# Turning ternary weight halves one at a time, and loading attention values earlier, in a two-layer transformer kernel

## The reference, cut to what matters

```python
xn = layernorm(x)
q, k = rope(xn @ wq), rope(xn @ wk)        # 16 query heads, 4 key heads of 128
s = softmax(mask(q @ k.T / sqrt(128))) @ v @ wo   # window of 64 keys and the first 32
gu = xn @ ternary(w_gate_up).T             # scale and sign per group of 64 weights
f = rms_norm(silu(gate) * up) @ ternary(w_proj).T
x = x + s * silu(f)
# then the second block: 16 heads of 16 over all 512 keys, and a GELU network in f16 products
```

## Time and profile before

| | us |
|---|---|
| median of 3 runs | 818.72 (818.72 to 818.73) |
| profiled execution, its own time | 823.13 |
| span of the profiled execution, first to last instruction | 821.3 |
| PE busy | 771.0 (94% of the span) |
| DVE, ACT, POOL busy | 607.8, 474.4, 299.4 |
| units of the first repetition (29.2 to 128.4): span | 99.2 |
| of it PE, DVE, ACT, POOL busy | 78.81, 79.54, 76.16, 67.73 |

### The profile page before, as it was taken

One profiled execution on the slowest core, in us unless ns is written; L12 is line 12 of the kernel. 1 busy time (PEld: TensorE's weight loads), 2 busy tenths in 40 slices (PEclk: granted clock), 3 DMA queues, 4 the chain that ended last, 5 costly groups with the idle time before them and its releaser, 6 DMA issues.

```text
span 821.3 us, 13360 instructions
## 1 busy us (share of the span) xinstructions
PE 771.0 (94%) x4656; PEld 476.8 (58%) x4656; DVE 607.8 (74%) x1632; ACT 474.4 (58%) x968; POOL 299.4 (36%) x255
## 2 busy tenths in 40 slices
PE   4869879989999999999999999999999999999996
PEld 2546568736446667856436667865445666774543
DVE  6949877758857677888957678687967667677862
ACT  3769764443777664143796775133696776233483
POOL 1348861122008885002006886001103888100201
PEclk9979989999999999999999999999999999999999
DMA  9131002184003120057002210028101300017400
GB/s 296 62 85 52 1 27 84 52 233 103 3 11 102 35 63 1 1 159 201 3 2 63 75 59 14 1 102 235 26 2 37 88 27 1 1 48 216 98 3 26
DMA packets 56818, 55.37 MB, mean 67 GB/s; under 512 B 14256, under 2 KB 43312, under 8 KB 56752
## 3 DMA queue, kind: packets, MB, share of 16 engines
q1 hardware_dynamic: 52768, 49.63, 21.3%
q10 hardware_dynamic: 3664, 3.84, 1.7%
q0 software_dynamic: 320, 1.05, 0.4%
HBM read 39.00 MB, written 15.24 MB: 66 GB/s over the span
## 4 chain that ended last, share of the span: by engine, by line
PE 68%; issue 11%; DVE 10%; ACT 4%; DMA 3%; POOL 2%; SPq 1%; ACTq 0%; POOLq 0%; DVEq 0%
PE bank L923 14%; PE bank L1034 7%; PE bank L958 6%; PE bank L1241 5%; PE bank L1225 5%; PE bank L1020 5%; PE bank L1136 4%; PE bank L1164 4%; PE bank L1208 3%; PE bank L1001 3%; PE bank L969 3%; PE bank L1213 2%; PE bank L983 2%; DVE mx L1597 1%; ACT region L760 1%
## 5 line engine op out<-in xcount | busy, mean ns | idle before, releaser
L1597 DVE TENSOR_REDUCE mx<-bank 128x1 f32<-128x512 f32 x256 | 161.1, 683 | 29.0 <-PE bank L1164 24.3
L603 POOL TENSOR_TENSOR region<-region 128x512 f32<-128x512 f32 x75 | 99.8, 1330 | 148.0 <-DVE region L1415 143.3
L923 PE MATMUL bank<-xnT,wrope 128*128 128x512 f32 x320 | 147.2, 603 | 3.3 <-ACT xnT L730 1.2
L875 ACT ACTIVATE region<-bank 128x512 f32<-128x512 f32 x256 | 132.9, 602 | 25.5 <-PE bank L1213 24.0
L760 ACT ACTIVATE region<-region,nb 128x128 f32<-128x128 f32 x256 | 81.5, 390 | 54.6 <-DVE nb L1427 54.3
L599 POOL TENSOR_TENSOR region<-region,sin_sb 128x512 f32<-128x512 f32 x60 | 84.5, 1408 | 41.7 <-ACT region L743 41.1
L923 PEld LDWEIGHTS bank<-xnT,wrope 128*128 128x128 f32 x320 | 58.7, 194 | 65.6 <-issue 61.5
L632 POOL TENSOR_TENSOR region<-region,bo_bc 128x256 f32<-128x256 f32 x16 | 11.7, 729 | 205.4 <-DVE region L1476 205.4
L1408 DVE TENSOR_TENSOR region<-bank,cos_sb 128x512 f32<-128x512 f32 x80 | 54.3, 686 | 36.5 <-PE bank L923 36.1
L741 ACT ACTIVATE region<-bank 64x512 f32<-64x512 f32 x80 | 47.6, 595 | 52.1 <-DVE region L1408 41.4
L958 PE MATMUL bank<-region 128*128 128x128 f32 x512 | 74.2, 290 | 1.6 <-ACT region L755 1.6
(11 more groups left out here) (144 smaller groups left out, 1347.7 us busy)
## 6 DMA issues: line engine op xcount, KB each, us to landing
wrope<-in_wrope SPq DMA_DIRECT2D x80, 128.0 KB, 2.2
scratch<-region SPq DMA_DIRECT2D x16, 512.0 KB, 5.2
Qp<-scratch SPq DMA_DIRECT2D x56, 128.0 KB, 3.6
Kp<-scratch SPq DMA_DIRECT2D x56, 128.0 KB, 3.9
scratch<-region SPq DMA_DIRECT2D x16, 256.0 KB, 5.6
X<-in_x SPq DMA_DIRECT2D x4, 512.0 KB, 4.1
out<-X SPq DMA_DIRECT2D x16, 128.0 KB, 2.0
VW<-v_rows SPq DMA_DIRECT2D x16, 102.0 KB, 2.8
```

The costliest lines, as they stand in the source:

```text
L603: nc.gpsimd.tensor_tensor(dst, dst, tiles(sw[:, r % 2, :], i), ALU.add)\
L875: nc.scalar.activation(P1[:, n % 8, :], turned_bank(n)[:, :], ACT.Exp, scale=SCALE1)\
L923: mm = nc.tensor.matmul(misc(b, name)[:, 0:width], lhs(c), xnT[:, c, :], start=(c == 0), stop=(c == DC - 1))
L1597: nc.vector.tensor_reduce(mx1[:, g % 2, column:column + 1], scores_bank(m)[:, :], AX.X, ALU.max)\
```

## The change

Everything lies in the first repetition; the amount of work is the same on every engine.

- The twelve half pieces were turned in pairs, in units 1, 3, 5, 8, 10 and 13. Now they are turned in eleven units, singly but for one pair: 0, 1, 3 (two), 6, 7, 9, 10, 11, 12, 13, 14.
- The sixteen gate and up products were dealt to units 4 to 13. Now they go to units 3 to 14: gate 0 in unit 3, up 0 in 4, gate 1 in 5, up 1 in 6, gate 2 and up 2 in 7, gate 3 in 8, none in 9, up 3 in 10, and the pairs 4 to 7 in units 11 to 14. So the bank turns change, too. PE's wait for turned weights is split: gate 0 and gate 4 wait for the two halves of their own piece, up 0 and up 4 for theirs.
- On SP, `load_piece(5)` with its wait stands behind the load of rotary weights 14 instead of 9, and so behind `load_windows`.
- On ACT, the four key copies of group 0 are no longer made behind the five swaps, `prepare(1)` and the halving of `bo`: the first is made ahead of swap 3, the second ahead of swap 4, the other two behind it. `key_windows` becomes `key_window`, which makes one copy; in other groups the four are made together as before.

```diff
     for s in range(NKV * TT):
         jobs += [("rope", r) for r in rope_at(s)] + ffn_at(b, s) + ([("ot", 0)] if s == OT_UNIT else [])
-        if b == 0 and s in TURN_UNITS:
-            jobs += [("wt", 2 * TURN_UNITS.index(s) + half) for half in range(2)]
+        jobs += [("wt", k) for k in TURN_AT.get(s, ())] if b == 0 else []
...
-FFN_FIRST = [0, 0, 0, 0, 1, 1, 2, 2, 1, 1, 2, 2, 2, 2, 0, 0]
+FFN_FIRST = [0, 0, 0, 1, 1, 1, 1, 2, 1, 0, 1, 2, 2, 2, 2, 0]
...
-TURN_UNITS = (1, 3, 5, 8, 10, 13)
+TURN_AT = {0: (0,), 1: (1,), 3: (2, 3), 6: (4,), 7: (5,), 9: (6,), 10: (7,), 11: (8,), 12: (9,), 13: (10,), 14: (11,)}
...
-                    if b == 0 and r == 9:
+                    if b == 0 and r == 14:
                         load_piece(5)
...
-            def key_windows(b, g):
-                act.wait_ge(rope_done.sem, rope_done.at(b, 5 * g + 1))
-                if g:
-                    act.wait_ge(s_full.sem, s_full.at(b, TT * g))
+            def key_window(b, g, k):
+                if k == 0:
+                    act.wait_ge(rope_done.sem, rope_done.at(b, 5 * g + 1))
+                    if g:
+                        act.wait_ge(s_full.sem, s_full.at(b, TT * g))
...
-            front(0)
+            xnT_copies(0)
+            for r in range(5):
+                if r >= 3:
+                    key_window(0, 0, r - 3)
+                swap(0, r)
+            for k in range(2, TT):
+                key_window(0, 0, k)
...
-                    for half in range(2) if b == 0 and s in TURN_UNITS else ():
-                        turned_weights(TURN_UNITS.index(s), half)
+                    for k in TURN_AT.get(s, ()) if b == 0 else ():
+                        turned_weights(k // 2, k % 2)
...
-                            if b == 0 and i % 4 == 0 and kind == "gate":
-                                pe.wait_ge(wt_freed.sem, wt_freed.at(0, 4 * (i // 4) + 4))
+                            if b == 0 and i % 4 == 0:
+                                pe.wait_ge(wt_freed.sem, wt_freed.at(0, 4 * (i // 4) + (2 if kind == "gate" else 4)))
...
-                    for half in range(2) if b == 0 and s in TURN_UNITS else ():
-                        turn_weights(TURN_UNITS.index(s), half)
+                    for k in TURN_AT.get(s, ()) if b == 0 else ():
+                        turn_weights(k // 2, k % 2)
```

More of the change, by code:

```diff
@@ L744, in swap @@
                     .then_inc(swap_done.sem, 1)
-            def key_windows(b, g):
-                act.wait_ge(rope_done.sem, rope_done.at(b, 5 * g + 1))
-                if g:
-                    act.wait_ge(s_full.sem, s_full.at(b, TT * g))
+            def key_window(b, g, k):
[3 more added lines that the diff above has]
+                        act.wait_ge(s_full.sem, s_full.at(b, TT * g))
                 keys = kT[:, g % 2, :]
-                for k in range(SPAN // QT):
+                if k < SPAN // QT:
                     src = keys[:, WIN + k * QT:WIN + k * QT + NWIN * QT].rearrange("p (n j) -> p n j", j=QT)
-                    nc.scalar.activation(kW[:, :, k * QT:(k + 1) * QT], src, ACT.Copy).then_inc(kw_ready.sem, 1)
-                front = keys[:, 0:FRONT].unsqueeze(1).broadcast_to([P, NWIN, FRONT])
-                nc.scalar.activation(kW[:, :, SPAN:P], front, ACT.Copy).then_inc(kw_ready.sem, 1)
+                    dst = kW[:, :, k * QT:(k + 1) * QT]
+                else:
+                    src = keys[:, 0:FRONT].unsqueeze(1).broadcast_to([P, NWIN, FRONT])
+                    dst = kW[:, :, SPAN:P]
+                nc.scalar.activation(dst, src, ACT.Copy).then_inc(kw_ready.sem, 1)
             def exps(b, u):
@@ L808, in _ @@
                     if s < NKV * TT:
-                        if s % TT == 0:
-                            key_windows(b, s // TT)
+                        for k in range(TT) if s % TT == 0 and (b or s) else ():
+                            key_window(b, s // TT, k)
                         for r in rope_at(s) if s == 0 else ():
```

## The result

| | before | after |
|---|---|---|
| median of 5 runs, us | 818.73 (818.72 to 821.08) | 815.04 (814.35 to 816.61) |
| ratio of the times, 95% interval | | 0.9937 (0.9917 to 0.9958) |
| profiled execution, own time | 823.13 | 815.04 |
| its span | 821.3 | 813.2 |
| start of unit 0 to the projection | 99.2 | 90.5 |

The change makes the kernel faster by 0.6%: by the ratio 5.2 us (3.4 to 6.8), by the medians 3.7. The forecast was 812.3, within 809.4 to 817.0. The two profiled executions differ by 8.1, which is more than the change is worth; why, the first experiment shows.

The account below looks back on a forecast made before the run. DVE was taken to pace the units, with PE's stalls costing its waits. Unit 4 earlier 3.3, gate 0 0.6 and fewer waits 2.8, less 0.3 for clock, gave −6.4 us: 818.7 to 812.3, range 809.4 to 817.0.

Parts of the forecast that it names:

- What bounds the kernel, and the end: First repetition: DVE paces the units, waiting 17.6 us for scores, rotary products and tanh; shifts pass to the program's end.
- The slack of product 7: Ahead of the projection: 3.9 us of slack is spent, and PE arrives about 7.5 us earlier, at 119.5 to 121.
- First term, 3.3 us: Unit 4: value-window stall gone, POOL's last sum of job 9 sets scores at 51.5, 3.3 us earlier.
- The 0.5 for one copy less: ACT, unit 1: one half piece copied ahead of prepare(2), not two, moves the chain to unit 4 forward 0.5 us.
- Key copies, 0: ACT, group 0: unit 1's scores come 1 us earlier, but DVE doesn't ask before about 35.5; gain 0.
- The dealing, 0.6 + 2.8, less 0.3: Units: gate 0 in idle time 0.6 us, DVE's waits from unit 4 to 14 down 2.8, less 0.3 for half clock.
- POOL and DVE, 0 with bounds of 1.0: Shared SBUF port: collisions of POOL and DVE instructions costed at 0, bounds ±1.0 us, one collision of 0.8 more or fewer.
- Clock: PE at unit 4: clock expected at half again after waits; full clock would give scores 0.9 us and rotary products 0.6.
- The spell that could not be placed: PE behind idle time in unit 7 or 11: one half-clock spell costing 1.0 to 1.9 us on PE, taken as 0.3.
- no dent but the first: Sign, PE's clock: the forecast is wrong if half-clock spells other than the first, at unit 4, show.
- rival 5: End of units: pair 7 in unit 14 puts 3.6 us ahead of the projection, making it slower; 820.0 us, chance 0.09.
- rival 3: Units 7 and 11: PE's clock falls, scores of 8 and 12 come 1.5 to 1.8 us late; 815.4 us, chance 0.20.

Follow-up runs that it names:

- the first experiment: The kernel before, unchanged, profiled and timed once more: span 819.0 us, median 821.7 us, ratio to before 1.0017.
- after again: The kernel after, unchanged, profiled and timed once more beside the kernel before: median 815.9 us, ratio to before 0.9931.
- before again: The kernel before, unchanged, in its second profiled execution and timing: median 821.7 us, ratio to before 1.0017.
- dealing only: The kernel before with only the two new tables (half pieces, products) and the split wait: median 817.1 us, ratio to before 0.9944.
- no SP move: The kernel after with load_piece(5) back behind rotary load 9, ahead of the value windows: median 815.5 us, ratio to before 0.9941.

## Why the prediction came out as it did

- **What bounds the kernel, and the end.** Right. The gain came from the stalls that DVE saw: those of the three kinds went from 17.6 us to 10.0. The remainder was as long as before to 0.4 us, but by luck: its first part was 1.0 shorter and its last 1.4 longer. The slack of product 7 was spent: projection at 119.86, for 119.5 to 121. The prediction's own figures don't quite meet here: a projection near 121 with the same remainder is 7.4 us, and it summed 6.4.
- **First term, 3.3 us.** Right in its releaser and nearly in its place (PE waits for L602; unit 4 at 50.75, for 51 to 52, and mask at 52.86, for 53.6 at half clock), wrong in its make-up and in what it is worth against a median. The sum was made against one execution and carried to the median with the words "all in all alike". They weren't alike: 2.4 us of that execution's excess lay in the landing that the change takes off the path. Against the kernel before with the quick landing, SP's part is 0.3 us at unit 4 and 0.1 at the projection. The 0.5 for one copy less measured 0.1. Two readings in it are off without a consequence: the wait of `load_piece(5)` ended when the rounding of piece 2 did (42.53 + 1.07 = 43.60), and not when it began; and L1445 moves as many bytes as the step that was estimated from it, not half.
- **Key copies, 0.** This step failed: they are worth 1.3 us. The prediction asked when DVE would want unit 1's scores, and found no reader. The reader was another one: the swaps of jobs 5 and 6 stand behind the copies on ACT, and through POOL they set swap 8, `prepare(2)`, swap 9 and unit 4. Of the 1.3, 0.84 is what these swaps gained, and most of the rest a sum of POOL's that met less of DVE's work. The rule of the prediction itself, that unit 4 hangs on POOL's job 9, had only to be followed two units further back.
- **The dealing, 0.6 + 2.8, less 0.3.** 3.1 forecast, 4.4 measured; right in kind, and the sizes off in two terms that partly cancel. Waits behind the mask of unit 4: for scores 0 as counted, for rotary products 4.3 and for tanh 3.0 (3.3 and 4.0 expected), together 7.3 as forecast; but DVE now also waits 0.9 for ACT's rounding of a piece, which was not in the sum, so 1.9 of the 2.8 came. Gate 0 gave its 0.7. Masks of units 8 and 12 stood at 80.55 and 105.86, for 80 and 105. In the execution of after again, with its dent in unit 11, 2.6 is left of the 4.4. How the dealing splits between single halves and the products' order stays open, as said above.
- **POOL and DVE, 0 with bounds of 1.0.** It came out at 1.0, the end of its bounds. DVE's groups between unit 4 and the projection, in the unchanged kernel's second profile (names, times | busy us, mean ns | idle before):

```profile
L1328 DVE TENSOR_TENSOR w1T<-w1T,H 128x1024 bf16<-128x1024 bf16 x4 | 7.3, 1820 | 0.1
...
L1464 DVE TENSOR_TENSOR region<-o_turned,rden 128x256 f32<-128x256 f32 x3 | 2.9, 970 | 0.1
```

and in the kernel after:

```profile
L1336 DVE TENSOR_TENSOR w1T<-w1T,H 128x1024 bf16<-128x1024 bf16 x4 | 6.4, 1607 | 0.1
...
L1472 DVE TENSOR_TENSOR region<-o_turned,rden 128x256 f32<-128x256 f32 x3 | 2.1, 684 | 0.1
```

These two groups, with as many instructions as before, take 1.7 us less (of the four L1328, three stood beside a POOL instruction and took 1.95 to 2.06 us; of the four L1336, two did, and the other two took 1.2); two steps of the ternary difference (L1331 and L1322) take 0.9 more, and the others together about 0.2 less, so the net gain is about 1.0. It is an arrangement of collisions that nobody chose. With 1.9 of the waits, 0.7 of gate 0 and the 0.6 of two masks that now stand behind the projection's start, 4.2 of the 4.4 are named.
- **Clock.** Right at unit 4 (half clock, scores 2.08 us). The spell that could not be placed is that of unit 11, and costs 1.2 to 1.4 us or nothing, by the execution; 0.3 was taken. By the prediction's own sign, no dent but the first, the first profile of the kernel after bears it out and the second doesn't.

Summed from unit 0 to the projection, the change is worth 5.9 us against the quick landing without the dent and 4.3 with it, against 6.4 forecast; the ratio says 5.2. Taken from the median of 818.7 this would be 813.5. The measured 815.0 is 1.5 above that, which fits with the runs of before that were shown: they were at the low end of its scatter. That the result lies near the forecast is in part luck. Against the trace that it was made from, the change gave 8.7 us to the projection and not 6.4, for the most part by the 1.3 of the key copies and the 1.0 of DVE's collisions; and 2.4 of the 8.7 was the late landing, which the other profiles with late windows don't have. The two errors, 2.3 and 2.4, cancel. No rival decided: pair 7 (rival 5) never got the chance to, and the clock (rival 3) took a share in one unit.

What stays open: why SP took 3.24 us to issue three of the loads in one execution and 1.49 in three others, and why a dent of the clock comes in some executions and not in others, in unit 11 as behind the units.

## What to carry to other kernels

Before a stall in a profile is priced, see a second execution: of a stall that ends with a DMA, a part can be that execution's own, and a sum carried to a median must leave that part out. When a copy or a transfer is moved and its own reader doesn't wait, follow what stood behind it on its engine, over other engines, to the next bound. And when PE is idle ahead of a stretch that others wait for, repeating harmless matmuls there can be worth something (1.9 us in one stage here), as long as the repeats end before the releaser does. Whether a dent costs anything is read a unit or two further on: that of unit 7 cost nothing, that of unit 11 1.2 to 1.4 us.

## What was not expected of the hardware

- The same four window loads, issued in the same order, landed 5.7, 5.5 and 5.5 us after the first issue in three profiles (before again, dealing only, no SP move), and 8.1 in the first. 1.75 of the 2.4 to 2.6 us lay in how long SP took to issue the first three (3.24 us against 1.49).
- After the same idle time of 2.2 us, at the same instruction of the same program, PE's clock stayed at full in one execution and was granted at 0.54 in another. That it falls after idling is what the Trainium skill ("TensorE: Matmul & The Clock Gate", part 1) says; these two executions show that the idle time alone didn't decide it. In the 3.8 us ahead of the wait PE worked without a pause in both.
- 3.8 us of repeated work on the engine that is busy 95% of the span made the kernel 0.3% faster (ratio 0.9900 beside 0.9931).
